# A four-layer decoder on one core: half of the shared features inside the first pipeline, input products inside the third, norms in two parts, and another order of loads

## The reference

```python
def _L1_ffn_ref(x, centroids, routing_bias, Wfc_r, Wproj_r, Wfc_sh, Wproj_sh):
    raw = jnp.einsum('bsd,ed->bse', x, centroids)
    ...
    h_sh = jax.nn.gelu(jnp.einsum('bsd,nfd->bsnf', x, Wfc_sh), approximate=False)
    shared_out = jnp.einsum('bsnf,ndf->bsd', h_sh, Wproj_sh)
    h_r = jax.nn.gelu(jnp.einsum('bsd,efd->bsef', x, Wfc_r), approximate=False)
    expert_out = jnp.einsum('bsef,edf->bsed', h_r, Wproj_r)
    routed_out = jnp.einsum('bsed,bse->bsd', expert_out, combine)
    return x + shared_out + routed_out

def _L3_ffn_ref(hidden_states, gru_w_ih, gru_w_hh, expr_w, ctx_w, ctx_b, ...):
    h0 = hidden_states.mean(axis=1) @ ctx_w.T + ctx_b
    xw = hidden_states @ gru_w_ih.T
    _, hs = jax.lax.scan(step, h0, jnp.swapaxes(xw, 0, 1))
    expr = (hidden_states @ expr_w.T).reshape(B, S, E, D)
    ...
```

## Time and profile before

| | |
|---|---|
| median of 3 runs | 3235.72 us (3233.26 to 3252.05) |
| profiled execution, its own time | 3258.05 us |
| span of the profiled execution | 3256.2 us |
| mean granted PE clock | 0.945 |
| PE / DVE / ACT / POOL busy | 92% / 48% / 23% / 7% of the span |

### The profile page before, as it was taken

How to read it: one execution, slowest core, us unless ns; L and a number is a source line. 1 busy time by engine, 2 the same in 40 slices (tenths; PEclk the granted TensorE clock), 3 DMA queues, 4 the chain that set the end, 5 groups by cost and what they waited for, 6 DMA issues and landing times.

```text
span 3256.2 us, 63316 instructions
## 1 busy us (share of the span) xinstructions
PE 2996.5 (92%) x25733; PEld 1697.8 (52%) x25733; DVE 1549.5 (48%) x4080; ACT 743.9 (23%) x1830; POOL 236.6 (7%) x433
## 2 busy tenths in 40 slices
PE   6888889889988999999889989999999999999897
PEld 4554456669755555555546643444444444444387
DVE  4645345411146566300564521466666666666643
ACT  2331133211122445211014411111111111111111
POOL 2001101020210000000200000000000000000011
PEclk8989989799988999999889979999999999999999
DMA  4000000258430000411000057000000000000176
GB/s 146 1 1 1 12 23 2 87 192 327 173 117 1 1 1 1 140 52 65 1 1 1 2 137 224 13 19 25 23 21 23 22 24 25 19 26 22 39 263 222
DMA packets 80720, 202.96 MB, mean 62 GB/s; under 512 B 32254, under 2 KB 55467, under 8 KB 67844
## 3 DMA queue, kind: packets, MB, share of 16 engines
q1 hardware_dynamic: 76568, 192.75, 18.0%
q0 software_dynamic: 3968, 7.56, 0.7%
HBM read 170.06 MB, written 37.53 MB: 64 GB/s over the span
## 4 chain that ended last, share of the span: by engine, by line
PE 81%; DVE 9%; DMA 4%; ACT 3%; issue 2%; POOL 1%; SPq 1%; another core or an unknown queue 0%; DVEq 0%; POOLq 0%; ACTq 0%
PE banks L1216 31%; PE banks L1036 9%; PE banks L868 4%; PE banks L588 4%; PE banks L762 3%; PE banks L541 3%; PE banks L1184 2%; PE banks L1101 2%; PE banks L1113 2%; PE banks L890 2%; PE banks L908 1%; PE banks L1263 1%; PE banks L914 1%; PE banks L930 1%; PE banks L657 1%
## 5 line engine op out<-in xcount | busy, mean ns | idle before, releaser
L1216 PE MATMUL banks<-arena 128*32 128x384 f32 x12800 | 1034.3, 486 | 1.9 <-DVE arena L2185 1.1
L1216 PEld LDWEIGHTS banks<-arena 128*32 128x32 f32 x12800 | 416.6, 110 | 613.7 <-issue 609.1
L1592 ACT ACTIVATE arena<-arena 128x256 f32<-128x256 f32 x200 | 83.4, 417 | 759.0 <-DVE arena L2197 759.0
L2197 DVE TENSOR_TENSOR arena<-banks,arena 128x256 f32<-128x256 f32 x200 | 84.9, 425 | 199.4 <-PE banks L1216 198.3
L1036 PE MATMUL banks<-arena 128*128 128x400 f32 x512 | 172.5, 499 | 1.5 <-DVE arena L2147 0.8
L868 PE MATMUL banks<-arena 128*100 128x256 f32 x512 | 151.7, 455 | 17.6 <-ACT arena L1517 5.3
L1327 ACT ACTIVATE arena<-banks 128x512 f32<-128x512 f32 (+2 forms) x120 | 68.5, 572 | 415.1 <-PE banks L1101 154.9
L588 PE MATMUL banks<-XNT,arena 128*128 128x400 f32 x384 | 151.2, 536 | 8.3 <-ACT XNT L1338 3.9
L762 PEld LDWEIGHTS banks<-arena 32*121 32x121 f32 x1536 | 105.7, 196 | 62.3 <-ACT arena L1436 47.3
L1036 PEld LDWEIGHTS banks<-arena 128*128 128x128 f32 x512 | 97.1, 190 | 76.8 <-DVE arena L2147 1.4
L1790 DVE TENSOR_REDUCE arena<-banks 100x4 f32<-100x1444 f32 x64 | 106.3, 1661 | 63.6 <-PE banks L718 63.5
(11 more groups left out here) (378 smaller groups left out, 4211.7 us busy)
## 6 DMA issues: line engine op xcount, KB each, us to landing
arena<-fc SPq DMA_DIRECT2D x22, 1024.0 KB, 4.7
arena<-pj SPq DMA_DIRECT2D x22, 1024.0 KB, 6.3
arena<-gu SPq DMA_DIRECT2D x21, 1024.0 KB
arena<-whh SPq DMA_DIRECT2D x32, 384.0 KB, 17.3
arena<-dn SPq DMA_DIRECT2D x21, 512.0 KB, 5.7
arena<-xw SPq DMA_DIRECT2D x400, 24.0 KB
xw<-arena SPq DMA_DIRECT2D x6, 1536.0 KB, 15.5
arena<-hh SPq DMA_DIRECT2D x16, 512.0 KB, 3.3
```

What stands on the lines that cost most here:

```text
L1216: last = nc.tensor.matmul(banks[32 * j:32 * j + 32, 2 * c + i, 0:384].rearrange("p (g n) -> p g n", g=3), hT[:, 1 - i, 32 * ub:32 * ub + 3 ...
L1592: nc.scalar.activation(rz[:, c, :], pre[:, c, :], ACT.Sigmoid).then_inc(sem["rz_done"], 1)
L2197: nc.vector.tensor_tensor(pre[:, c, :].rearrange("p (g n) -> p g n", g=2), banks[:, 2 * c + i, 0:2 * P].rearrange("p (g n) -> p g n", g=2) ...
```

## The change

The functions stay; what moves is which work is called in which round.

- **Early features.** Eight units (block m of the features for the first 400 tokens, m = 0 to 7) are computed in pipeline A's items 38 to 40 (`early_unit`), into banks 6 and 7. DVE copies units 0 to 5 to `early_h`, ACT takes 6 and 7 through Gelu and then does the Gelu of the six. After the pipeline PE does the router's scores of four batches, the `down` rows of batch 0, the transposes, the other four batches' scores, 4 + 4 units, and the other 7 batches.
- **Loads.** The shared expert's second matrix is loaded during pipeline A, not after it. In the tile transfers the order is up(0), down(0), up(2), down(2), up(1), rows 0 to 2, down(1). Biases and context of pipeline B are loaded after the 20 tiles and not ahead of them.
- **The sort** has 9 matmuls, of up to 72 columns, in the place of 16.
- **Norms.** The statistics are made known after the third and after the fourth batch of a group, and POOL does 12 short operations and three normalisations, and then 12 and one.
- **Kind "first".** The scores of the next item stand ahead of the second weighted half; ACT and not DVE copies the first half of the values (`own_values`).
- **Input products.** `DRAINED = 3` of the 7 tiles are computed in pipeline C's items 15 and 16 (`drain_unit`, 18 units of 128x512), tokens in the order batch, token and no longer token, batch. `XNT`, `xw`, `shown` and the loads of the GRU follow that order. The expressions of a lap come in 10 loads of 8 rows where there was one of 80. Tiles 0 and 1 are stored, and `ctx_w` and 4 of the 32 parts of `whh` are loaded, ahead of pipeline C's end; the other 28 parts now change partition group with every part.

```diff
+        DRAINED = 3
+        def drain_units(i, r):
+            return {(15, r): range(2 * r, 2 * r + 2), (16, 0): range(8, 11), (16, 1): range(11, 14), (16, 2): range(14, 16), (16, 3): range(16, 18)
+                    }.get((i, r), ())
+        def early_units(i, r):
+            return {(38, 1): (0,), (38, 3): (1,), (39, 0): (2,), (39, 1): (3,), (39, 2): (4,), (39, 3): (5,), (40, 0): (6, 7)}.get((i, r), ())
...
+            def early_unit(m):
+                if m == 0:
+                    wait("l_shared", 16)
+                    need("A", "xT", len(KINDS["A"]), 0, 1)
+                u, full_ = open_m("A", "shared", m)
+                for kk in range(C):
+                    last = nc.tensor.matmul(u[:, 0:HALF], up_w[1][:, kk, m * P:m * P + P], XNT[:, kk, 0:HALF], start=kk == 0, stop=kk == C - 1)
...
+                        if then == "first" and r == 0:
+                            score_round(ph, i + 1, 0)
                         if past == "first" and r == 0:
                             weighted_half(ph, i - 1, 1)
-                        if then not in (None, "mixture", "wide") and (r == 0 or then == "cross"):
+                        if then not in (None, "first", "mixture", "wide") and (r == 0 or then == "cross"):
                             score_round(ph, i + 1, r)
...
-            pe.wait_ge(sem["l_shared"], 16)
-            features(up_w[1], range(0, 8, 2))
+            pe.wait_ge(sem["l_rb"], 32)
+            router_rows("a", range(4))
+            pe.wait_ge(sem["l_shared"], 32)
+            pe.wait_ge(sem["gelu"], 2 * B + 1)
+            shared_row(0)
             turn_rest("A")
-            pe.wait_ge(sem["l_rb"], 32)
-            router_rows(cent[:, :].rearrange("p (k e) -> p k e", k=C))
+            router_rows("d", range(4, B))
             features(up_w[1], range(1, 8, 2))
             sort_pairs(0)
-            MARK["shared1_up"] = features(up_w[1], range(8, 16))
+            MARK["shared1_up"] = features(up_w[1], range(9, 16, 2))
             evacuated("a")
-            pe.wait_ge(sem["l_shared"], 32)
-            down(h0T, down_w[1], 8)
+            for b in range(1, B):
+                shared_row(b)
...
-            pe.wait_ge(sem["l_gru"], 16)
-            input_gates(0)
+            input_gates(DRAINED)
...
-            for i in range(1, TILES):
+            for i in range(DRAINED + 1, TILES):
                 input_gates(i)
...
-                if b % 4 == 3:
-                    x, y = stats[:, b - 3:b + 1, 7], rstd[:, b - 3:b + 1]
+                if b % 4 >= 2:
+                    some = slice(b - 2, b + 1) if b % 4 == 2 else slice(b, b + 1)
+                    x, y = stats[:, some, 7], rstd[:, some]
...
-                pool.wait_ge(sem["known"], norms_before(ph, s, g) + 1)
-                four = slice(4 * g, 4 * g + 4)
+                for part, (lo, hi) in enumerate(((4 * g, 4 * g + 3), (4 * g + 3, 4 * g + 4))):
+                    pool.wait_ge(sem["known"], 2 * norms_before(ph, s, g) + part + 1)
...
-                for t in range(2):
+                for t in (0, 2):
                     load_up(stage, t)
                     load_down(stage, t)
+                load_up(stage, 1)
                 sp.wait_ge(sem["l_sorted"], 16 * 16 * (stage + 1))
                 for t in range(3):
                     load_rows(stage, t)
+                load_down(stage, 1)
...
-            parts = [(j, c, v) for j in range(4) for c in range(2) for v in range(4)]
+            parts = [(j, c, v) for c in range(2) for v in range(4) for j in range(4) if 4 * c + v != early_whh]
...
-            x_rows = xw.rearrange("(s b) (j g u) -> s j b g u", b=B, j=4, g=3)
+            x_rows = [xw[2 * k:T + 2 * k].rearrange("(b s) (j g u) -> s j b g u", b=B, j=4, g=3) for k in range(2)]
```

274 lines of the change are left out of this document (175 added, 99 removed).

## The result

| | before | changed |
|---|---|---|
| median | 3243.89 us (3233.26 to 3261.18, 6 runs) | 3200.6 us (3194.56 to 3202.62, 6 runs) |
| profiled execution, its own time | 3258.05 us | 3194.56 us |
| mean granted PE clock in it | 0.945 | 0.961 |

The ratio is 0.9865 (95% interval 0.9842 to 0.9888): 43 us less, with 47 forecast. 3200.6 lies inside the range of the forecast (3158 to 3218) and just above its middle part (3180 to 3200). The changed kernel, run again with other runs of before, gave 3199.8 us and 0.9867 (0.985 to 0.9885).

The account below looks back on a forecast made before the run. PE, busy 92% of the span, was taken as the bound, but transfers in the input section. Terms 5 - 9 - 2 - 25 + 2 - 18 = -47 us: 3258 to 3211 profiled, 3189 median; range 3158 to 3218.

Parts of the forecast that it names:

- Layer 1 behind the pipeline (-25): From pipeline A's end to the first turned pairs: fewer features and waits, 78.1 us down to about 53, -25 us (-29 to -14).
- rival 2: Behind pipeline A: DVE stands still until POOL's scatter is over, so PE loses 12 us more; 3201 us, chance 0.16.
- End of C and the input section (-18): Pipeline C's end to the GRU: early products and stores leave fewer bytes in a transfer-bound section, -18 us (-34 to -10).
- the phase's end moves by 2.5: Pipeline C's end: eleven added units ahead of the last out product delay it by only 2.5 us, with the clock restored.
- Norms (-9): Pipelines' norms in two parts: PE waits less for POOL in four places, 16.0 us before; -9 us (-5 to -13).
- Kind "first" (+5): Pipeline A's first items: the copy behind ACT's Gelu delays PE's turned maxima 0.7 us in seven items, +5 us (0 to +6).
- A's last slots (-2): Pipeline A's last items: eight early feature units, 11 us of work, fit into low-clock gaps; -2 us (-6 to +5).
- Loads of B (+2): Pipeline B's biases and context, loaded behind the tiles, run beside POOL's gathers: +2 us (0 to +5).
- Rival 1: Input section becomes bound by PE, transfers hold 291 GB/s and the clock returns more fully: 3176 us, chance 0.24.
- Rival 3: GRU: scattered token rows and nine more loads a lap make each step pay, about 3279 us (slower), chance 0.06.
- Rival 4: Slots in A and C are not free: early and drained units cost their full price, 3220 us, chance 0.08.

## Why the prediction was right, and where it was not

**The total.** -47 forecast, -43 measured, inside the range. It is right in that the gain lies where it was put, in the two large terms; that it is met within 4 us is partly luck. The sum was made against the profiled execution, 3258 to 3211, and the changed kernel's profile has 3194.56, 16 us less; the median of the kernel before moved from 3235.72 (3 runs) to 3243.89 (6 runs), and to the former it would be -35. Several terms below missed in opposite directions. (The ends of the terms, which I gave as -85 and -10, add up to -82 and -13.)

**Layer 1 behind the pipeline (-25): right in its mechanism, and 53 us by two misses that cancel.** The waits for rows (6.4) and half the features are gone, PE is busy for 46.45 of the 48.1 us. PE and the scatter do arrive together: the last scatter is issued at 669.19, the rows are there at 676.3, 0.17 us after PE, and both some 5 us ahead of the forecast. What was left to PE I had at 51.2 us busy (66.07 less 14.2 and 0.7), which keeps the clock of before, 0.87; it is 46.45, at 0.96. The other miss is rival 2: with the wait for the rows gone, rows that come late count in full. The six profiles that have this part unchanged (both of the changed kernel, norms in one part, no drained units, old order of the parts, old form of "first") take 48.1, 51.8, 54.7, 54.7, 57.7 and 57.7 us, 54.1 in the mean. The rival gave it 12 us at a chance of 0.16; it is in five of six profiles, with 4 to 10 us. Its mechanism as I put it, DVE standing still until the scatter is over, does not fit: in most profiles DVE takes up single rows in between, and ACT is late as well.

**End of C and the input section (-18): right in kind, too small.** From the end of the last out product to the GRU it is 95.6 us, where it was 124.1; the sum had 101.5 for 122.9. From 1876.5 to 1954 us the DMA engines are full (the row stands with the order of the parts). 77.5 us at 279 GB/s are 21.6 MB, where I had 21.3 MB and 81.6 us. The rate was mis-sized: I kept 261 for the new mix, and the slow start of before (150 and 199 GB/s from 1916 to 1928 us, now 209 and more in the like place) was part of the 261. The tail was mis-sized by as much, 14.1 us instead of 18.4; the wait that ends at its start is now one for a store of `shown`, where before it was one for a store of `xw`. The bytes came out by luck. I had put the stores of tiles 0 and 1 ahead of the section, as the part on the change does, and only tile 0's is:

The changed kernel, timeline of SP:

```profile
1874.88 0.36 SPq L2903 DMA_DIRECT2D xw<-arena  x1
```

The last out product ends at 1872.46, so these 1.57 MB stayed in; and the 1 MB of `ctx_w`, which is gone from the section, I had not taken off. The step "the phase's end moves by 2.5" nearly held: the last out product ends 66.9 us behind C's middle transposes, 63.5 in the profile of before and 61.8 in the other two.

**Norms (-9): the waits right, the gain wrong.** I took each us of PE's wait as a us of time. 9.3 of 16 us of waits went; A as a whole lost 1 to 6 us of it again to the clock. What failed is the step from a shorter wait to a shorter time, where nothing behind it was shown to stay at its clock. In the changed kernel the net is 0 to 3 us, by the stretches and by the ratios 0.9872 and 0.9866. In the kernel before, to which the sum was made, two parts alone gave 6 us (0.9982), within the bounds of 5 to 13, though with an interval that takes in 0.

**Kind "first" (+5): mechanism right for one item, term wrong.** 0.46 an item and not 0.7, since the out product now starts 0.37 us behind the maxima in place of 0.60. The term for the stretch left out the clock, and with it the mean of the stretch is 3 us shorter with the new form, not 5 longer.

**A's last slots (-2): within the bounds** (-0.5), and bunching the same units shows what the gaps were worth. **Loads of B (+2)**: not to be seen beside 198 to 204 us for that stretch in either kernel.

**Rival 1** (transfers faster, PE the bound) has its first half: 279 for 291 GB/s; PE did not become the bound: it still waits 5.9 us once for ACT, which waits for a store. **Rival 3** (the GRU pays) is out: 1037.9 us in every profile, old order and new. **Rival 4** is out: PE's 11 us of added work cost nothing in A's slots, and of its 31 us in C the eleven units ahead of the last out product, 19 us of work, cost 3.3 to 5.1; with the seven behind it the way to the last transposes is 10 to 12 us longer (79.6 for 69.3 and 67.6).

## What to carry to other kernels

Work that has to be done anyway, put one piece at a time into the gaps of a stage that runs at a low granted clock, costs next to nothing; the same pieces in a row cost most of their price (7 of 11 us here). A wait that is removed inside a pipeline is not yet time gained: one that was 3.9 us shorter was followed by a stretch 6 us longer. Check the granted clock of the stretch behind it, and take differences of single profiles only beside the mean clock of each. In a section bound by transfers count the bytes ahead of the event that ends it, and take the rate from a stretch with the mix that will be left.
